# Masked adapters for pair 0, tables spread by ones products, and fp32 adapter products in column groups

## The reference

```python
# layer 0: dense plus a low-rank adapter chosen per sequence (8 adapters of rank 16)
x = x + (x @ W.T + (x @ A[idx0].T) @ Bm[idx0].T * scalings[idx0])
# layer 1: a 64x64 matrix of 200, chosen per sequence, mixes the tokens
x = x + einsum('bct,bcd->bdt', x, w1[idx1])
# layer 2: causal attention, 16 heads of 32, q scaled by min(cond, 4) per sequence
x = x + attention(x, cond, Wq, Wk, Wv, Wo)
# layer 3: as layer 1, with one of 8 matrices
x = x + einsum('bct,bcd->bdt', x, w3[idx3])
```

## Time and profile before

| | |
|---|---|
| median of 3 executions | 654.2 us (651.0 to 654.92) |
| profiled execution, its own time | 654.01 us |
| its span, first to last instruction | 652.3 us |
| TensorE busy | 627.8 us, 96% of the span |
| VectorE busy | 392.0 us, 60% |
| ScalarE busy | 217.3 us, 33% |
| GpSimd busy | 140.3 us, 22% |
| mean granted TensorE clock | 0.992 |

### The profile page before, as it was taken

The page is one execution under the profiler, slowest core; times in us unless marked ns, Lnnn a source line. Parts: engine busy times, 40 slices in busy tenths (PEclk is TensorE's granted clock), DMA queues, the critical chain, the costliest instruction groups (busy, mean ns, idle before and its releaser), DMA issues.

```text
span 652.3 us, 19480 instructions
## 1 busy us (share of the span) xinstructions
PE 627.8 (96%) x7684; PEld 531.2 (81%) x7684; DVE 392.0 (60%) x542; ACT 217.3 (33%) x411; POOL 140.3 (22%) x113
## 2 busy tenths in 40 slices
PE   4899999999999999999999999999999999999897
PEld 3697887979888797988879798887979888797784
DVE  2567676555666655566665567656556765655363
ACT  2534342332333233233323223332232333222222
POOL 1005031140403104040310404032040402204031
PEclk8899999999999999999999999999999999999999
DMA  8440201102030110203011020301103020100101
GB/s 281 140 121 19 54 7 59 42 14 78 4 88 8 56 40 12 81 4 88 8 56 40 10 82 4 87 9 52 44 8 85 4 79 18 42 23 0 39 2 65
DMA packets 41770, 31.90 MB, mean 49 GB/s; under 512 B 16014, under 2 KB 31374, under 8 KB 41742
## 3 DMA queue, kind: packets, MB, share of 16 engines
q1 hardware_dynamic: 37790, 25.49, 14.1%
q10 hardware_dynamic: 3952, 6.03, 2.8%
HBM read 22.58 MB, written 8.91 MB: 48 GB/s over the span
## 4 chain that ended last, share of the span: by engine, by line
PE 91%; DVE 4%; issue 1%; DMA 1%; ACT 1%; ACTq 1%; POOL 0%; SPq 0%; DVEq 0%
PE banks L487 9%; PE banks L492 9%; PE banks L488 9%; PE banks L464 5%; PE banks L513 5%; PE banks L539 5%; PE banks L581 5%; PE banks L588 5%; PE banks L582 5%; PE banks L439 4%; PE banks L441 4%; PE banks L443 4%; PE banks L517 4%; PE banks L515 4%; PE banks L531 4%; PE banks L555 3%
## 5 line engine op out<-in xcount | busy, mean ns | idle before, releaser
L1122 POOL TENSOR_TENSOR probs<-probs,row_max 128x1024 f32<-128x1024 f32 x32 | 61.0, 1905 | 328.7 <-DVE row_max L966 328.7
L487 PE MATMUL banks<-x1T_hi,w_hi 128*128 128x256 f32 x512 | 130.4, 287 | 0.1
L488 PE MATMUL banks<-x1T_hi,w_lo 128*128 128x256 f32 x512 | 128.2, 283 | 0.0
L487 PEld LDWEIGHTS banks<-x1T_hi,w_hi 128*128 128x128 f32 x512 | 98.0, 191 | 1.6 <-DVE w_lo L893 0.3
L488 PEld LDWEIGHTS banks<-x1T_hi,w_lo 128*128 128x128 f32 x512 | 98.1, 192 | 0.0
L492 PE MATMUL banks<-x1T_lo,w_hi 128*128 128x256 f32 x512 | 82.3, 283 | 0.0
L492 PEld LDWEIGHTS banks<-x1T_lo,w_hi 128*128 128x128 f32 x512 | 70.6, 192 | 0.0
L952 DVE TENSOR_TENSOR qkT<-banks,beta 128x512 f32<-128x512 f32 x32 | 22.0, 691 | 58.5 <-PE banks L492 58.5
L970 DVE TENSOR_REDUCE row_sum<-probs 128x16 f32<-128x1024 f32 x32 | 39.0, 1220 | 25.7 <-ACT probs L793 25.7
L513 PE MATMUL banks<-w_hi,x1T_hi 128*128 128x512 f32 x128 | 51.6, 403 | 1.4 <-issue 0.2
L439 PE MATMUL banks<-w_hi,xT_hi 128*128 128x512 f32 x128 | 50.6, 396 | 1.0 <-DVE w_lo L893 1.0
(11 more groups left out here) (103 smaller groups left out, 1110.5 us busy)
## 6 DMA issues: line engine op xcount, KB each, us to landing
x_in<-in_x_dram SPq DMA_DIRECT2D x60, 128.0 KB, 2.7
out_dram<-x_y SPq DMA_DIRECT2D x15, 512.0 KB, 2.8
b_sel<-b_parts SPq DMA_DIRECT2D x192, 32.0 KB, 1.7
w_in<-in_L_cond_weights_dram SPq DMA_DIRECT2D x128, 16.0 KB
probsT<-in_L_cond_W_dram ACTq DMA_DIRECT2D x1, 1024.0 KB, 10.1
probs<-in_L_cond_Wk_dram ACTq DMA_DIRECT2D x1, 1024.0 KB, 8.1
qkT<-in_L_cond_Wq_dram ACTq DMA_DIRECT2D x1, 1024.0 KB, 10.2
probsT<-in_L_cond_Wv_dram ACTq DMA_DIRECT2D x1, 1024.0 KB, 6.4
```

The costliest lines, as they stand in the source:

```text
L487: nc.tensor.matmul(out_ap, w_hi[:, w, c, cols], x1T_hi[:, c, :], start=(c == 0), stop=False)
L488: nc.tensor.matmul(out_ap, w_lo[:, w, c, cols], x1T_hi[:, c, :], start=False, stop=False)
```

## The change

1. Pair 0's adapters. TensorE multiplies all eight adapters at once (`first_adapters_down`: 4 fp32 products, 128 rows of A by 256 tokens), VectorE multiplies the result with a mask `chosen` (which adapter is the sequence's own), and `first_adapters_up` adds 6 F32R products of 512 columns with the whole `b_hi`, `b_lo`. `select_a(0)`, `gather_b` of pair 0 and the three-part placing of pair 0 are gone.
2. Tables. `scal`, `cond` and the four first indices are loaded as one row each, and `spread_rows` multiplies them with a row of ones (3 small fp32 products) into bank 1; VectorE makes `scal_rows`, `chosen` and `beta` of that with a few small operations. The two repeating DMAs are gone.
3. Order. TensorE turns A first, then W0, then Bm. SyncE issues the DMA of A second instead of third, the w1 gather and the load of x for pair 1 earlier. `load_w(WQ)` and `load_w(WV)` stand later on ScalarE. `beta` is made ahead of `take_matrix(WV)`, and TensorE waits for it behind the first key part. `select_a(1)` stands ahead of `copy_k(0)`.
4. `adapters_down` of pairs 1 to 15 is fp32: `a_sel` has 64 columns and no hi and lo parts, `xT` is read unsplit, and each product has 32 stationary columns and 128 moving ones, on one of four groups of 32 array columns. `xa_low`, `xa_sum`, `xa` and `xa_hi` have 128 columns instead of 256.
5. In the last step `copy_pT(i, 1)` stands ahead of `copy_y(i - 1)`.

```diff
+            def first_adapters_down():
+                pe.wait_ge(turned_lo, GROUP_A + 1)
+                pe.wait_ge(first_copied, TILES)
+                for c in range(NC):
+                    last = nc.tensor.matmul(bank[XA_FIRST][:, 0:PT], a_all[:, c, :], xT[:, c, :],
+                                            start=(c == 0), stop=(c == NC - 1))
+                last.then_inc(xa_mm, 1)
+            def first_adapters_up():
+                pe.wait_ge(turned_lo, GROUP_B + 1)
+                pe.wait_ge(xa_first_split, 1)
+                for t in range(TILES):
+                    for xa_part, b_part in ((xa_first_hi, b_hi), (xa_first_hi, b_lo), (xa_first_lo, b_hi)):
+                        last = nc.tensor.matmul(bank[MIX[t]][:], xa_part[:, tok(t)], b_part[:],
+                                                start=False, stop=xa_part is xa_first_lo)
+                    last.then_inc(x0_mm, 1)
             def adapters_down(i):
-                pe.wait_ge(a_ready, i + 1)
-                pe.wait_ge(xT_split, i + 1)
+                pe.wait_ge(a_ready, i)
+                pe.wait_ge(x_turned, i)
+                n = SEQT * RANK
                 for c in range(NC):
-                    for part in (xT_hi, xT_lo):
-                        last = nc.tensor.matmul(bank[DOWN][:, 0:PT], a_sel[:, c, :, :].rearrange("p a n -> p (a n)"),
-                                                part[:, c, :], start=(c == 0 and part is xT_hi),
-                                                stop=(c == NC - 1 and part is xT_lo))
+                    for t in range(TILES):
+                        at = (c % 2 * TILES + t) * n
+                        last = nc.tensor.matmul(bank[DOWN][at:at + n, 0:P], a_sel[:, c, t * n:(t + 1) * n],
+                                                xT[:, c, tok(t)], start=(c < 2), stop=(c >= 2))
                 last.then_inc(xa_mm, 1)
...
-            pe.wait_ge(b_ordered, 1)
-            turn(GROUP_B, [b_nat[:, c, :] for c in range(NC)], in_rows_of_b)
+            pe.wait_ge(consts_step, 13)
+            spread_rows()
             pe.wait_ge(a_loaded, 16)
             turn(GROUP_A, [every_fourth(a_nat, c) for c in range(NC)])
             for c in range(NC):
                 if c == NC - 1:
-                    pe.wait_ge(xT_split, 1)
+                    pe.wait_ge(first_copied, TILES)
                 turn_part(W0, c)
+            pe.wait_ge(b_ordered, 1)
+            turn(GROUP_B, [b_nat[:, c, :] for c in range(NC)], in_rows_of_b)
             for c in range(NC):
                 pe.wait_ge(turned_lo, GROUPS_OF[W0][c] + 1)
                 for t in range(TILES):
                     layer0_part(t, c)
                 if c == 0:
-                    adapters_down(0)
+                    first_adapters_down()
                 else:
                     turn_part(WK, c - 1)
-            adapters_up(0)
+            first_adapters_up()
...
                 key_part(0, m)
-                if m > 0:
+                if m == 0:
+                    pe.wait_ge(tables_done, PSEQ)
+                else:
                     turn_part(WV, m)
...
                 copy_pT(i, 0)
+                if not nxt:
+                    copy_pT(i, 1)
                 if prev:
                     copy_y(i - 1)
```

More of the change, by code:

```diff
@@ L425, in turn_first_x, with spread_rows @@
                     last.then_inc(xT_mm, 1)
+            def spread_rows():
+                pe.wait_ge(idx0_cast, 1)
+                pe.wait_ge(scal_loaded, 16)
+                pe.wait_ge(cond_loaded, 16)
+                at = 0
+                for row in (cond_row, scal_row, idx0_first):
+                    n = row.shape[1]
+                    last = nc.tensor.matmul(bank[ROWS][:, at:at + n], one_row[:], row[:], start=True, stop=True)
+                    at += n
+                last.then_inc(rows_mm, 1)
@@ L748, in select_a @@
                     at = act.value_load(idx0_row[0:1, bass.ds(i * PSEQ + n, 1)], min_val=0, max_val=ADAPTERS - 1)
-                    last = copy(a_sel[:, :, :, n * RANK:(n + 1) * RANK], a_all[:, :, :, bass.ds(at * RANK, RANK)])
+                    last = copy(a_sel[:, :, n * RANK:(n + 1) * RANK], a_all[:, :, bass.ds(at * RANK, RANK)])
                 last.then_inc(a_ready, 1)
@@ L753, in xa_low_part @@
                 act.wait_ge(xa_mm, i + 1)
-                copy(xa_low[:], bank[DOWN][half(1), 0:PT]).then_inc(xa_low_done, 1)
+                copy(xa_low[:], bank[DOWN][half(1), 0:P]).then_inc(xa_low_done, 1)
             def xa_hi_part(i):
-                act.wait_ge(xa_scaled, i + 1)
+                act.wait_ge(xa_scaled, i)
                 copy(xa_hi[:], xa[:]).then_inc(xa_hi_done, 1)
-                act.wait_ge(xa_hi_done, i + 1)
+                act.wait_ge(xa_hi_done, i)
                 if not (isinstance(i, int) and i == 0):
@@ L764, in xa_hi_part @@
                     for part in (0, 2):
-                        last = copy(xa_parts[part * n:(part + 1) * n, t, :], xa_hi[t * n:(t + 1) * n, tok(t)])
+                        last = copy(xa_parts[part * n:(part + 1) * n, t, :], xa_hi[t * n:(t + 1) * n, :])
                 last.then_inc(xa_hi_placed, 1)
@@ L848, in _ @@
             load_w(WK, Wk)
+            for t in range(TILES):
+                act.wait_ge(first_lo_done, t + 1)
+                copy(xT[:, :, tok(t)], in_chunks(bank[SC[t]])).then_inc(first_copied, 1)
+            take_hi(GROUP_A, a_all[:, 0:2, :], in_chunks(bank_of_group(GROUP_A))[:, 0:2, :])
+            load_w(WQ, Wq)
+            take_matrix(W0)
             act.wait_ge(turned, GROUP_B + 1)
-            act.wait_ge(scal_loaded, 16)
+            act.wait_ge(scal_step, 2)
             nc.scalar.activation(b_hi[:], bank_of_group(GROUP_B), ACT.Copy,
                                  scale=scal_rows[:, 0:1]).then_inc(turned_hi, 1)
-            load_w(WQ, Wq)
-            take_hi(GROUP_A, a_all[:, :, 0, :], in_chunks(bank_of_group(GROUP_A)))
-            act.wait_ge(turned_lo, GROUP_A + 1)
-            act.wait_ge(idx0_loaded, 16)
-            select_a(0)
-            take_matrix(W0)
+            act.wait_ge(xa_first_masked, 1)
+            copy(xa_first_hi, xa_first).then_inc(xa_first_hi_done, 1)
             load_w(WV, Wv)
-            xa_low_part(0)
-            xa_hi_part(0)
             for c in range(3):
@@ L874, in _ @@
             x_hi(1)
+            act.wait_ge(turned_lo, GROUP_A + 1)
+            act.wait_ge(idx0_loaded, 16)
+            select_a(1)
             copy_k(0)
-            select_a(1)
             xa_low_part(1)
@@ L926, in xa_lo_part @@
                     rows = slice(t * n, (t + 1) * n)
-                    last = rest(xa_parts[n:2 * n, t, :], xa[rows, tok(t)], xa_hi[rows, tok(t)])
+                    last = rest(xa_parts[n:2 * n, t, :], xa[rows, :], xa_hi[rows, :])
                 last.then_inc(xa_lo_placed, 1)
```

159 lines of the change are left out of this document (104 added, 55 removed).

## The result

The changed kernel takes 645.84 us (median of 4 runs, 645.02 to 647.52) where the kernel before took 653.16 us beside it (4 runs, 651.00 to 654.92): ratio 0.9893, 95% interval 0.9854 to 0.9932, so 7.3 us less. Each ratio further down is against runs of the kernel before that were taken beside that experiment; where one profile is compared with another, each is a single execution. The profiled execution has a span of 644.2 us; the one of before had 652.3.

A forecast was written before the change was run, and what follows sets the result against it. TensorE was taken to bound the loop, VectorE step 0. Start-up +0.6, step 0 -0.6, pairs -0.2 and last step -1.6 gave -1.8 us, forecast 652.3 us; range 648.5 to 656.5 (0.84).

The forecast's parts named there:

- Part 2: Start-up up to layer 0: W0's transposes start at 12.8 us, layer 0 at 17.1; net -0.8 us.
- The second branch of that part: Start-up: if A and its small rows land no earlier, VectorE's work on them comes first and W0's transposes start at 13.2 us.
- Part 3: Start-up, first_adapters_down: the dearer fp32 product spends the head start, +0.2 us by its end; bounds -1.1 and +1.0.
- If the rise stays at 21.3 us: Start-up, first_adapters_down: with the clock rising at 21.3 us as before, the product is done at 22.3 us.
- the nearer bound: Start-up, first_adapters_down: the clock rises already at 17.9 us because TensorE has no gap; product done at 21.0, -1.1 us.
- rival 2: Start-up: the clock rises with the closed gap, layer 0's chunks and all behind come 1.3 us earlier, 650.0 us; chance 0.22.
- Part 4: Start-up, first_adapters_up to the first scores: four more products mostly in slack; first scores +0.6 us, bounds -1.0 and +3.
- Parts 1, 5 and 6: Looped pairs: -0.2 us in all; step 0: earlier mask, -0.6 us; last step: swapped copies, attention directly behind layer 3, -1.6 us.
- part 1: Looped pairs: adapter product lies in a wait allowing about 1.15 us, so 0.02 us at most in each of 14 pairs.
- rival 4: Looped pairs: each gains what the adapter product gets shorter, 0.45 x 15 = 7 us, giving 645 us; chance 0.05.

## Why the prediction was wrong

**Part 2 failed, and it failed at the landings.** It took W0's landing ("about 11.9") and A's (10.44, less 0.8) from rows in which the repeated scaling was running ahead of A, though the change takes that transfer away; it was never priced. A landed at 5.0 and W0 at 10.4, and W0's transposes began at 11.26 instead of 12.8: 1.5 us. A's landing is the scaling's doing: 3.7 us from issue without it, 8.1 with it alone. W0's goes with the repeated conditions, the other transfer that the change takes away: 10.8 to 11.9 in the six traces with them, 10.1 to 10.6 in the eight without. The 11.9 that the sum used was the latest of the six. Both landings had to come early, since W0's identity stands behind A's half on VectorE. The second branch of that part (A late, 13.2) is what the two experiments with the scaling back measured, 13.6 and 13.9.

**Part 3 failed at "If the rise stays at 21.3 us".** The clock rose at 16.3. Counted from W0's first transpose that is 5.1 us, where the sum took 8.5 (21.3 less 12.8) and the nearer bound had 5.1 (17.9 less 12.8). With the 1.3 us that rival 2 gave an early rise and the 1.5 of the landings the forecast of the first scores would have been 47.0; they came at 46.52. The traces give (us; the clock's column is where its record has the upper level begin, and the lengths of the products agree):

| kernel | W0's first transpose | clock at its upper level | first scores | first transpose to rise | to first scores |
|---|---|---|---|---|---|
| before | 13.25 | 21.34 | 49.19 | 8.1 | 35.9 |
| before, copies swapped | 14.44 | 18.79 | 48.67 | 4.4 | 34.2 |
| before, code moved | 13.81 | 18.10 | 48.02 | 4.3 | 34.2 |
| after | 11.26 | 16.32 | 46.52 | 5.1 | 35.3 |
| after, both repeating DMAs | 13.93 | 18.91 | 49.19 | 5.0 | 35.3 |
| after, W0 behind Bm | 11.88 | 17.57 | 46.97 | 5.7 | 35.1 |

The first three have the same stream of products there and a gap ahead of layer 0 (0.96, 0.41 and 0.74 us), and rise after 4.3 to 8.1 us; the last three have no gap and take 5.0 to 5.7. So the gap is not what decides, and rival 2's mechanism isn't borne out: kernels with a gap rose as early as those without one. The execution that I read, the kernel before's, had the longest of the three gaps, but the kernel with A ahead of the scaling, with the same stream of products and a gap of 0.94, rose after 3.1 us (at 16.65). So its rise was simply a late one. From the first three, a rise later by 3.7 us costs 1.7, an estimate of 0.46 us a us. (The fourth kernel doesn't fit it: it takes 35.2 to the first scores in spite of its early rise, and where it loses the rest isn't known.) Set to a rise after 4.3 us, the changed kernel would take 34.9 from the transpose to the scores, 0.7 more than before: the dearer first products cost roughly what parts 2 to 4 had for them (37.0 forecast against 35.9, +1.1). The size was right, the clock was not. By the same estimate the change itself gave 1.3 us at the first scores (2.0 at the transposes less that 0.7), and the other 1.4 of the 2.7 come from the two rises, above all from the late one of before. What decides the moment of the rise stays open.

**Part 4** was right apart from what it inherited: from layer 0's second chunk to the first scores 27.7 us were measured, 27.5 forecast, 27.1 before.

**Not in the prediction at all: the hole in step 14.** It stood in the profile of before, and I went from the looped step to the last without reading the unrolled steps between. The sum put everything between them at nothing. The code theory would have told that an edit of TensorE's code moves it, with 2.6 us to win there or as much to lose in another step. That it went was luck: nothing in the change aims at it, and two other shifts of the code moved it away in one kernel and into two steps in the other. It was the second largest piece of the result, and the range had no term for it.

**Parts 1, 5 and 6 were right.** The product is 0.57 us to the next instruction where nothing waits behind it (0.5 to 0.7 forecast), the wait behind it holds, the step gained 0.04; only the room in the wait was over-sized (1.15 for 0.95); step 0 gave -0.8 for a forecast of -0.6, its mask following the scores by 0.13 us; the last step -1.7 for -1.6. What part 1 held against the Trainium skill's rule stands as the runs have it (its row of 512 columns in 0.24 us is one of the start-up, though, and not of a looped step): products that use all 128 rows overlapped fourfold in separate column groups, and not at all in one.

The 8.05 us of the profiles against the forecast 1.8: 3.3 in the start-up, 2.6 in step 14, 0.3 in step 0 and the end. The measured time lies beside rival 4's 645 by chance: that rival wanted 0.45 us from each pair, and the step gave 0.04.

## What to carry to other kernels

When a change removes a transfer, price what ran beside it and behind it on its queue, not the transfer itself: half a kilobyte in 4-byte elements was worth 2.3 us at the first transposes. Before costing edits one by one, list the holes of the old trace that are put down to nothing (issue), since an edit of that engine's code can move them, and see how far the times of the runs spread; judge an edit to the loop by the length of a looped step, not by the kernel's time. A product shortened ahead of a wait is worth nothing until the wait goes; remove both together and measure them together: here 641.7 us, 12.5 less than the kernel before beside it.

## What the runs showed of the hardware that I had not expected

- Code arrives in pieces of some 16 KB: the queue of the transfer beside the hole has 19 of them, 0.31 MB in all, in the profile's page after. The attention's 128 products and their 128 weight loads run in 1.5 us, and a piece took 1.3 us in the kernel before. With one under way among them, TensorE stood 1.0 to 2.2 us; that the hole is a wait for this code is inferred from the transfer's place and from the two experiments that move nothing but code. The Trainium skill, "Runtime: NRT & Kernel Launch", section Instruction fetch mechanics, says that the cost of crossing such a boundary is mostly hidden; if the holes are these crossings, the runs show the contrary for bursts of small products.

```profile
q8 instruction: 19, 0.31, 0.2%
```

- Behind most of these holes the granted clock fell to 0.50 while TensorE was busy again, though not in the profile of before. A hole with the fall cost its step 3.4 to 3.9 us (41.7 to 42.1 us against 38.2 to 38.3), the one of before without it 2.4.
- Four column groups of full-height fp32 products run side by side: 0.65 us for 16 passes against 1.93 in one group.
